# Tokens times the fused matrix: seven block products for each pair of token blocks in place of eight

## The chip, the cores and the metric

The kernel runs on one core of one Trainium2 chip. The metric is the device time of one execution in microseconds (us), the median of three runs. The core's engines are named as the profile names them: PE (TensorE, its matmuls) with PEld (its weight loads), DVE (VectorE), ACT (ScalarE), POOL (GpSimd) and SP (SyncE, which here issues nearly all DMAs).

## The reference, cut to what matters

Four residual layers follow one another on x, 32 sequences of 64 tokens of 1024 values. Every layer adds a linear map of the tokens, chosen or adapted by an index of the sequence:

```python
x = x + _L0_cond_ref(x, itok_B_0_15, L0_cond_weights)            # mixes the 64 tokens of a sequence, W = weights[index]
x = x + _L1_cond_ref(x, itok_B_0_15, L1_cond_W, lora_A, lora_B)  # x W1 + (x A[i]) B[i], rank 16
x = x + _L2_cond_ref(x, itok_B_0_2, L2_cond_W, lora_A, lora_B_w) # x W2' + (x A[j]) B' / 2, rank 32
x = x + _L3_cond_ref(x, itok_B_0_7, L3_cond_W, Wr, A, B)         # x W3' + gated low rank, top 2 of 8 experts
```

All layers but the gate are linear in x. The kernel uses this: it multiplies the weights together first and the tokens once by the result.

## The kernel before

**Number format.** Every fp32 operand of a matmul is kept as two fp32r tiles, `_hi` (ACT copies with rounding) and `_lo` (DVE subtracts `_hi` from the value). A product takes the three terms of `TERMS`: hi by hi, hi by lo, lo by hi.

**Front (to about 262 us).** From W2 and W3 (and A3, Wr beside it) the kernel makes the operand E, and from W1 and E the fused matrix M of 1024 x 1024 with the columns TB for the low-rank parts. This second product goes row block by row block (`rows`, ten of them: two of LoRA B, then eight of W1). One row block has three chunks of columns, 488, 448 and 384 wide, each into its own PSUM bank; ACT and DVE take each chunk out as hi and lo, directly into M and TB. The last row block's chunks end at about 252.6, 257.4 and 261.5 us.

**Token blocks (262 us to the end).** A block is 128 tokens, two sequences; there are 16. Two blocks (s = 0, 1) make one turn of the loop on every engine; the first two and the last two are written out. For each block PE runs:

- the wide product, 48 matmuls of 512 columns: two column halves, eight blocks of K, three terms, into banks 0 and 1 (`run`, L965);
- the narrow product for the next block, 24 matmuls of 232 columns, block by S, the columns of TB and of A1 chosen for the two sequences (`narrow`, L951). POOL's `select` chooses them by index;
- the mixing of tokens by BD (layer 0), of the narrow result (L977) and of the wide one (L1014), and small matmuls and transposes for the low-rank chain h1, h2, gates (L983 to L1002);
- sixteen matmuls of 512 columns that add it all up in banks 2 and 3 (L1009 to L1021).

ACT and DVE take results out of PSUM (`xm`, `xn`, `h1c`, `h2c`, gates), and copy the output to `ost`. SP, one queue in order, loads the tokens (`raw`), BD (`load_w0`), stores the output and loads `b1s`, the rows of LoRA B of the two sequences, from DRAM (`load_b1s`; the index is read into a register first). Each engine's order is the order of the code; semaphores alone tie them.

## Time and profile before

| | before |
|---|---|
| time, median of 3 runs | 560.11 us (560.01 to 560.23) |
| span of the profiled execution | 558.3 us |
| PE busy | 551.1 us, 99% of the span |
| DVE, ACT, POOL busy | 199.2, 133.7, 77.3 us |
| granted TensorE clock | full in all slices |

The profile times the span from the first to the last instruction of one execution; the timed runs are 1.8 us longer, which lies around the span. The profile gives each matmul of 512 columns some 0.40 us, but matmuls overlap: the distance from one start to the next says what one costs, and is read from the timeline.

### The profile page before, as it was taken

What the parts mean: (1) busy time and instruction counts of PE and PEld (TensorE: products, weight loads), DVE (VectorE), ACT (ScalarE), POOL (GpSimd) and SP (SyncE); (2) the same over time, 40 slices, a digit from 0 to 9 for tenths busy, and PEclk for the clock granted to TensorE, in tenths of its full rate; (3) what the DMA queues carried; (4) which work ended last, traced back from release to release, by engine and by line L of the source; (5) the groups of instructions that cost most, each with busy time, mean ns of one, the idle gap of its engine ahead of it and who ended that gap; (6) DMA issues with size and microseconds to landing.
All of it is one profiled execution on the core that took longest, in us unless ns stands there. A gap on an engine that the chain in (4) does not pass through costs nothing.

```text
span 558.3 us, 9078 instructions
## 1 busy us (share of the span) xinstructions
PE 551.1 (99%) x2898; PEld 491.9 (88%) x2898; DVE 199.2 (36%) x566; ACT 133.7 (24%) x274; POOL 77.3 (14%) x202
## 2 busy tenths in 40 slices
PE   7999999999999999999999999999999999999997
PEld 6999999999999999999888888888888888888885
DVE  4751312132322222213543344334444344435423
ACT  5541311121111111113222212221222122221211
POOL 2401000000000000004122122202220222022200
PEclk9999999999999999999999999999999999999999
DMA  8703020044131101001522132223312232223211
...
DMA packets 21834, 45.37 MB, mean 81 GB/s; under 512 B 8100, under 2 KB 12836, under 8 KB 21684
## 3 DMA queue, kind: packets, MB, share of 16 engines
...
q14 instruction: 10, 0.08, 0.1%
...
## 4 chain that ended last, share of the span: by engine, by line
PE 97%; DMA 1%; DVE 0%; SPq 0%; ACT 0%; issue 0%; POOL 0%
PE bank L965 32%; PE bank L931 26%; PE bank L889 19%; PE bank L951 8%; PE bank L1021 4%; PE bank L1014 4%; PE bank L1009 1%; PE bank L1010 1%; DMA w2raw<-in_w_dram 1%; PE bank L977 1%; PE bank L983 0%; PE bank L991 0%; PE bank L1002 0%; PE bank L987 0%; DVE w2s_lo L670 0%; ACT w2s_hi L542 0%
## 5 line engine op out<-in xcount | busy, mean ns | idle before, releaser
L965 PE MATMUL bank<-m_lo,xt_hi 128*128 128x512 f32 x256 | 103.0, 403 | 0.0
L965 PE MATMUL bank<-m_hi,xt_lo 128*128 128x512 f32 x256 | 101.3, 396 | 0.0
L965 PE MATMUL bank<-m_hi,xt_hi 128*128 128x512 f32 x256 | 100.2, 391 | 0.0
L931 PE MATMUL bank<-e_lo,w1t_hi 128*128 128x488 f32 (+2 forms) x240 | 86.9, 362 | 0.0
L931 PE MATMUL bank<-e_hi,w1t_hi 128*128 128x488 f32 (+2 forms) x240 | 86.8, 362 | 0.0
L931 PE MATMUL bank<-e_hi,w1t_lo 128*128 128x488 f32 (+2 forms) x240 | 86.7, 361 | 0.0
L889 PE MATMUL bank<-g_hi,w2s_hi 128*128 128x384 f32 (+1 forms) x192 | 64.7, 337 | 2.4 <-DVE w2s_lo L670 2.4
L889 PE MATMUL bank<-g_hi,w2s_lo 128*128 128x384 f32 (+1 forms) x192 | 64.5, 336 | 0.0
L889 PE MATMUL bank<-g_lo,w2s_hi 128*128 128x384 f32 (+1 forms) x192 | 64.5, 336 | 0.0
L965 PEld LDWEIGHTS bank<-m_lo,xt_hi 128*128 128x128 f32 x256 | 48.1, 188 | 10.7
L965 PEld LDWEIGHTS bank<-m_hi,xt_hi 128*128 128x128 f32 x256 | 48.3, 189 | 8.9
L965 PEld LDWEIGHTS bank<-m_hi,xt_lo 128*128 128x128 f32 x256 | 48.2, 188 | 8.6
L931 PEld LDWEIGHTS bank<-e_lo,w1t_hi 128*128 128x128 f32 x240 | 45.2, 188 | 3.9
L931 PEld LDWEIGHTS bank<-e_hi,w1t_hi 128*128 128x128 f32 x240 | 45.0, 188 | 4.0
L931 PEld LDWEIGHTS bank<-e_hi,w1t_lo 128*128 128x128 f32 x240 | 45.1, 188 | 3.9
L670 DVE TENSOR_TENSOR xm_lo<-bank,xm_hi 128x512 fp32r<-128x512 f32 x32 | 22.1, 692 | 72.2 <-ACT xm_hi L616 72.2
L670 DVE TENSOR_TENSOR m_lo<-bank,m_hi 128x384 f32 (+3 forms) x24 | 12.3, 513 | 83.8 <-ACT tb_hi L583 57.5
L889 PEld LDWEIGHTS bank<-g_hi,w2s_hi 128*128 128x128 f32 x192 | 36.0, 188 | 3.1 <-issue 3.1
L951 PE MATMUL bank<-s_hi,xt_hi 128*128 128x232 f32 x128 | 36.3, 283 | 0.0
L889 PEld LDWEIGHTS bank<-g_hi,w2s_lo 128*128 128x128 f32 x192 | 36.0, 188 | 0.0
L889 PEld LDWEIGHTS bank<-g_lo,w2s_hi 128*128 128x128 f32 x192 | 36.0, 188 | 0.0
L951 PE MATMUL bank<-s_lo,xt_hi 128*128 128x232 f32 x128 | 35.2, 275 | 0.0
...
## 6 DMA issues: line engine op xcount, KB each, us to landing
...
```

Source lines behind the costliest of these rows:

```text
L670: V.tensor_tensor(dst, src, f32(hi), ALU.subtract).then_inc(signal, 1)
L889: ins = nc.tensor.matmul(to[:, 0:w], lhs, G[c][z][:, k, 0:w], start=(k == 0 and n == 0), stop=(k == K - 1 and n == len(terms) - 1), skip_g ...
L931: ins = nc.tensor.matmul(stage_bank(u, j)[:, 0:WIDTH[c]], W1T[u][a][:, k, :], EX[c][z][:, k, :], start=(k == 0 and (a, z) == TERMS[0]), st ...
L951: ins = nc.tensor.matmul(bank[4][:, 0:SC], XT[s][a][:, k, :], S[z][:, k, :], start=(k == 0 and (a, z) == TERMS[0]), stop=(k == K - 1 and ( ...
L965: ins = nc.tensor.matmul(bank[c][:, :], XT[s][a][:, k, :], M[z][:, k, c * BANK:(c + 1) * BANK], start=(k == 0 and (a, z) == TERMS[0]), sto ...
L977: ins = nc.tensor.matmul(res[:, 0:SC], BD[s][a][:, :], XN[z][:, :], start=(a, z) == TERMS[0], stop=(a, z) == TERMS[-1], skip_group_check=True)
L1009: nc.tensor.matmul(bank[2 + c][:, :], h1T[:, :], b1s[s][:, halves[c]], start=True, stop=False, skip_group_check=True)
L1010: nc.tensor.matmul(bank[2 + c][:, :], h2T[:, :], b2s[:, halves[c]], start=False, stop=False, skip_group_check=True)
L1014: nc.tensor.matmul(bank[2 + c][:, :], BD[s][a][:, :], XM[z][:, halves[c]], start=False, stop=False, skip_group_check=True)
L1021: ins = nc.tensor.matmul(bank[2 + c][:, :], GHT[a][:, :], B3[z][:, halves[c]], start=False, stop=(a, z) == TERMS[-1], skip_group_check=True)
```

## The change

Token blocks are now taken in pairs b0, b1. Tokens (b0, b1) by the halves of K, and M by halves of K and of columns, are 2 x 2 blocks, and their product is made by Strassen's scheme in the form with fewer sums (Winograd's). Each of the seven products p1, p5, p6, p2, p7, p3, p4 is 12 matmuls (four blocks of K, three terms) of 512 columns.

- The right operands are b11, b21, b22 of M and four combinations t1 to t4. Row blocks of M leave PSUM unsplit (`rows_raw`), POOL forms the combinations from them in SBUF (`right_of`, `combine`), and ACT and DVE split the seven operands in pieces of up to 2048 columns after the last row's first chunk (`split_hi`, `split_lo`).
- The left operands are the two blocks and sums of their halves: POOL makes four sums of 512 columns for each pair in the tile `tmp` and in `raw[1]` (`first_sum`, `pair_sums`), ACT and DVE split each (`operand_hi`, `operand_lo`). The tiles are reused: CS is t1's and t3's left operand, then XM slot 0; XB's first half is also XM slot 1; `ost` 2 and 3 lie in XB.
- Three sums of products are made by DVE in PSUM between accumulations (`bank[BB]`, `bank[BD_]`, `bank[BC]`), with p1 and p5 copied to SBUF by ACT (`held_p1`, `held_p5`).
- The output is made tile by tile, four tiles of 128 x 512 for each pair, on two banks in turn; `b1s[0]` is needed by the tiles 0 and 1 of the last four steps of PE's pair. SP stores each tile, and loads b1s[0] of the next pair behind the store of tile 1, b1s[1] behind that of tile 3. A load of b1s is four DMAs, not eight, from a scratch copy with three parts.
- S keeps its layout, but the columns chosen by `select` come from unsplit TBA, so POOL splits them (two copies and two subtractions of 256 columns in place of four copies).

```diff
+            def pair_io(p, last):
...
+                    for s in range(2):
+                        sp.wait_ge(s_idx, 48)
+                        sp.wait_ge(s_bd, 2 * p + s + 1)
...
+                    for s in range(2):
+                        sp.dma_start(raw[s][:, :, :], x[bass.ds(2 * p + 2 + s, 1)].rearrange("a p k t -> p (a k) t")).then_inc(s_raw[s], 16)
+                for n, (s, c) in enumerate(TILES):
+                    sp.wait_ge(s_idx, 48)
+                    if n % 2 == 0:
+                        sp.wait_ge(s_ya, 2 * p + n // 2 + 1)
+                    else:
+                        sp.wait_ge(s_yd, 2 * p + n // 2 + 1)
+                    sp.dma_start(orows[bass.ds(2 * p + s, 1)].rearrange("a t d -> (a t) d")[:, c * BANK:(c + 1) * BANK], ost[n][:, :]
+                                 ).then_inc(s_st[n], 16)
+                    if n % 2 and not last:
+                        done = held(sp, 4 * p + n + 1)
+                        sp.wait_ge(s_idx, 48)
+                        sp.wait_ge(s_y, done)
+                        load_b1s(2 * p + 2 + s, s)
...
             pool.wait_ge(s_acc, ACC_A + ACC_B - 2)
+            pool.wait_ge(s_rd, 3 * LAST + 2)
+            pool.wait_ge(s_ra, 4 * LAST + 2)
             select(0)
-            diagonal(0, 0)
-            pool.wait_ge(s_acc, ACC_A + ACC_B - 1)
-            for s in range(2):
-                nc.gpsimd.memset(f32(b1s[s][:, D + C3:]), 0.0).then_inc(s_b1z, 1)
-            diagonal(0, 1)
-            pool.wait_ge(s_accl, ACC_A + OUT * (ROWS - 1) + OUT_AT[1])
...
+            row_there(LAST)
+            right_of(2, KH - 1)
+            pool.wait_ge(s_acc, ACC_A + ACC_B)
+            first_sum(0)
+            right_of(4, KH - 1)
+            nc.gpsimd.memset(f32(b1s[0][:, D + C3:]), 0.0).then_inc(s_b1z, 1)
+            pool.wait_ge(s_s0l, 1)
+            nc.gpsimd.memset(f32(b1s[1][:, D + C3:]), 0.0).then_inc(s_b1z, 1)
+            right_of(3, KH - 1)
+
+            def pair_sums(p, last):
+
+                r11, r12, r21 = raw[0][:, 0:KH, :], raw[0][:, KH:K, :], raw[1][:, 0:KH, :]
+                pool.wait_ge(s_raw[0], 16 * p + 16 * (ROWS // 2 + 1))
+                pool.wait_ge(s_opl, OPS * p + 2)
+                nc.gpsimd.tensor_tensor(tmp[:, :, :], tmp[:, :, :], r11, ALU.subtract).then_inc(s_sum, 1)
+                if isinstance(p, int) and p == 0:
+                    select(1)
+                pool.wait_ge(s_opl, OPS * p + 3)
+                nc.gpsimd.tensor_tensor(tmp[:, :, :], r12, tmp[:, :, :], ALU.subtract).then_inc(s_sum, 1)
+                pool.wait_ge(s_opl, OPS * p + 4)
+                nc.gpsimd.tensor_tensor(r21, r11, r21, ALU.subtract).then_inc(s_sum, 1)
+                if not last:
+                    select(2 * p + 2)
+                    first_sum(p + 1)
+                    select(2 * p + 3)
+                    diagonal(2 * p + 2, 0, 4 * p + 2)
+                    diagonal(2 * p + 3, 1, 4 * p + 4)
...
+                act.wait_ge(s_sum, 4 * p + 2)
+                if not first:
+                    act.wait_ge(s_st[0], 16 * p)
+                    act.wait_ge(s_st[1], 16 * p)
+                operand_hi(DS[0][:, :, :], tmp[:, :, :])
+                h1_t(b0, 0)
...
+                nc.scalar.activation(held_p1[:, :], bank[BA][:, :], ACT.Copy).then_inc(s_cp, 1)
+                act.wait_ge(s_raw[1], 16 * p + 16 * (ROWS // 2 + 1))
+                if first:
+                    act.wait_ge(s_tr, formed(3, KH - 1))
+                else:
+                    act.wait_ge(s_mix, 4 * p)
+                    act.wait_ge(s_st[2], 16 * p)
+                    act.wait_ge(s_st[3], 16 * p)
+                operand_hi(XB[0][:, :, :], raw[1][:, :, :])
+                if first:
...
+                act.wait_ge(s_wide, made + PRODUCT["p5"])
+                nc.scalar.activation(held_p5[:, :], bank[BC][:, :], ACT.Copy).then_inc(s_cp, 1)
+                act.wait_ge(s_sum, 4 * p + 4)
+                operand_hi(CS[0][:, :, :], raw[1][:, 0:KH, :])
+                if first:
+                    split_hi("b22", WHOLE)
+                exp_of(b0)
+                xn_hi(b1, YB)
+                act.wait_ge(s_sum, 4 * p + 3)
+                operand_hi(XB[0][:, 0:KH, :], tmp[:, :, :])
...
+            act.wait_ge(s_ra, 4 * KH)
+            act.wait_ge(s_rd, 3 * KH)
+            split_hi("b11", WHOLE)
+            act.wait_ge(s_tr, formed(1, KH - 1))
+            split_hi("t1", WHOLE)
+            act.wait_ge(s_rd, 3 * LAST + 1)
+            nc.scalar.activation(S[0][:, :, 0:C3], TBC[:, :, :], ACT.Copy).then_inc(s_s0h, 1)
+            rows_raw(ROWS - 1, 1, [1])
+            left_hi(0)
+            act.wait_ge(s_tr, formed(2, KH - 2))
+            split_hi("t2", FRONT)
+            act.wait_ge(s_ra, 4 * LAST)
+            act.wait_ge(s_rd, 3 * LAST)
+            split_hi("b21", FRONT)
+            split_hi("t3", FRONT)
+            rows_raw(ROWS - 1, 1, [2])
+            act.wait_ge(s_b2st, 16 * 3)
+            xn_hi(0, YB)
+            pair_hi(0, False)
+            with act.Fori(1, NP - 1) as p:
...
+
+                operand_lo(CS[1][:, :, :], tmp[:, :, :], CS[0][:, :, :], ops + 2)
+                if first:
+                    dve.wait_ge(s_tr, formed(4, KH - 1))
+                    split_lo("t2", BACK, SPLIT_HI["t2b"])
+                first_low_rank(b0, 0, steps)
+                operand_lo(DS[1][:, :, :], tmp[:, :, :], DS[0][:, :, :], ops + 3)
+                if first:
+                    split_lo("b21", BACK, SPLIT_HI["b21b"])
+                second_low_rank(b0, 0, steps)
+                operand_lo(XB[1][:, :, :], raw[1][:, :, :], XB[0][:, :, :], ops + 4)
+                if first:
+                    dve.wait_ge(s_tr, formed(3, KH - 1))
+                    split_lo("t3", FRONT, SPLIT_HI["t3a"])
+                route(b0, 0, steps)
+                operand_lo(CS[1][:, :, :], raw[1][:, 0:KH, :], CS[0][:, :, :], ops + 5)
+                dve.wait_ge(s_wide, made + PRODUCT["p6"])
+                dve.wait_ge(s_cp, 2 * p + 1)
+                V.tensor_tensor(bank[BB][:, :], bank[BB][:, :], held_p1[:, :], ALU.add).then_inc(s_add, 1)
+                if first:
+                    split_lo("t3", BACK, SPLIT_HI["t3b"])
+                dve.wait_ge(s_add, 3 * p + 1)
+                dve.wait_ge(s_cp, 2 * p + 2)
+                V.tensor_tensor(bank[BD_][:, :], bank[BB][:, :], held_p5[:, :], ALU.add).then_inc(s_add, 1)
+                gates(b0, 0, steps)
+                if first:
+                    split_lo("b22", WHOLE, SPLIT_HI["b22"])
+                xn_lo(b1, YB)
+                operand_lo(XB[1][:, 0:KH, :], tmp[:, :, :], XB[0][:, 0:KH, :], ops + 6)
+                first_low_rank(b1, 1, steps)
...
+            def tile(p, n, first, last):
+
+                s, c = TILES[n]
+                to, cols = bank[YB + n % 2], slice(c * BANK, (c + 1) * BANK)
+                above(pe, s_yd if n % 2 else s_ya, 2 * p + n // 2)
+                if n == 1 and not last:
+                    pe.wait_ge(s_xnl, 2 * p + 3)
+                pe.wait_ge(s_xml, 4 * p + n + 1)
+                for a, z in TERMS:
+                    ins = nc.tensor.matmul(to[:, :], BD[s][a][:, :], XM[n % 2][z], start=(a, z) == TERMS[0], stop=False, skip_group_check=True)
+                ins.then_inc(s_mix, 1)
+                nc.tensor.matmul(to[:, :], h1T[s][:, :], b1s[s][:, cols], start=False, stop=False, skip_group_check=True)
+                nc.tensor.matmul(to[:, :], h2T[s][:, :], b2s[:, cols], start=False, stop=False, skip_group_check=True)
+                pe.wait_ge(s_ghl, 2 * p + s + 1)
+                if first and n == 0:
+                    pe.wait_ge(s_b3l, 1)
...
+                there("b11")
+                part("p1", 0, 5)
+                mixed(b0, 0)
+                part("p1", 5, 11)
+                h1_across(b0, 0)
+                part("p1", 11, 12)
+                pe.wait_ge(s_opl, OPS * p + 2)
+                there("t1b")
+                part("p5", 0, 3)
+                h1_into(b0, 0, p)
+                part("p5", 3, 11)
+                h2_across(b0, 0)
+                part("p5", 11, 12)
+                pe.wait_ge(s_opl, OPS * p + 3)
+                there("t2b")
+                part("p6", 0, 4)
                 if first:
...
+                h2_into(b0, 0)
+                part("p6", 4, 12)
+                pe.wait_ge(s_opl, OPS * p + 4)
+                narrow(b1, XB, YB)
+                pe.wait_ge(s_cp, 2 * p + 1)
+                there("b21b")
+                part("p2", 0, 6)
+                mixed(b1, 1)
+                part("p2", 6, 12)
+                gated_across(b0, 0)
+                pe.wait_ge(s_add, 3 * p + 2)
+                pe.wait_ge(s_opl, OPS * p + 5)
+                there("t3b")
+                part("p7", 0, 1)
+                h1_across(b1, 1)
+                part("p7", 1, 6)
+                h1_into(b1, 1, p)
+                part("p7", 6, 12)
+                pe.wait_ge(s_opl, OPS * p + 6)
+                there("b22")
+                part("p3", 0, 2)
+                h2_across(b1, 1)
+                part("p3", 2, 8)
+                h2_into(b1, 1)
+                part("p3", 8, 12)
+                pe.wait_ge(s_add, 3 * p + 3)
+                there("t4")
+                part("p4", 0, 12)
...
+            pe.wait_ge(s_rd, 3 * LAST + 3)
+            pe.wait_ge(s_ra, 4 * LAST + 2)
+            pe.wait_ge(s_ml, SPLIT_LO["b11"])
+            pe.wait_ge(s_s0l, 1)
+            pe.wait_ge(s_opl, 1)
+            nc.tensor.matmul(bank[BD_][:, :], XA[0][:, 0, :], MO["b11"][0][:, 0, :], start=True, stop=True, skip_group_check=True)
+            narrow(0, XA, YB)
```

Where POOL's program passes from the front to the token blocks, it had this order before (behind two reads of `idx_a` S is filled for block 0, then BD, then the spare columns of b1s are cleared):

```order
L475 ISA [waits s_id]
L475 COPY s_hi<-a1raw 128x8x16
L475 ISA
L475 COPY s_hi<-a1raw 128x8x16
L485 TENSOR_TENSOR s_lo<-a1raw,s_hi 128x8x16 [waits s_a1c,s_id]
L485 TENSOR_TENSOR s_lo<-a1raw,s_hi 128x8x16
L456 TENSOR_TENSOR bdraw_100<-bdraw_100,ident 128x128 [waits s_w00]
L461 CAST bd_hi<-bdraw_100 128x128 [waits s_bdc,s_id]
L463 TENSOR_TENSOR bd_lo<-bdraw_100,bd_hi 128x128 [waits s_bdc]
L496 MEMSET b1s_132 96x64 [waits s_acc]
```

and has this now, behind four reads of `idx_a` and `idx_l` and two copies from `tba` (`tba` holds the unsplit columns, `mr_left`, `mr_right` and `tr` the parts of M and t1 to t4, `tmp` the tokens' sum):

```order
L527 COPY s_hi<-a1raw 128x8x16
L527 ISA
L527 COPY s_hi<-a1raw 128x8x16
L531 TENSOR_TENSOR s_lo<-tba,s_hi 128x8x32 [waits s_a1c,s_id]
L531 TENSOR_TENSOR s_lo<-tba,s_hi 128x8x32
L531 TENSOR_TENSOR s_lo<-a1raw,s_hi 128x8x16 x2
L534 TENSOR_TENSOR tr_54<-mr_right,tr_53 128x512 [waits s_tr,s_rd,s_ra]
L556 TENSOR_TENSOR tmp<-raw_115 128x512 [waits s_raw1,s_acc]
L534 TENSOR_TENSOR tr_56<-mr_left,tr_54 128x512 [waits s_tr]
L580 MEMSET b1s_161 96x64
```

Two index reads became four, the first `select` fills and splits all columns of S, and b1s is cleared only behind three operations of 512 columns.

SP's order at the end of a block before (one store, then b1s for the block after the next one, which is used a whole block later):

```order
L400 DMA out_dram<-ost_96 128x1024 [waits s_yfree1,s_yfree0]
L349 TENSOR_LOAD idx_a
L349 ISA x2
L349 TENSOR_LOAD idx_l
L349 ISA x2
L366 ISA
L366 DMA b1s_132<-b1scr 32x1160
L366 ISA
L366 DMA b1s_132<-b1scr 32x32
L366 DMA b1s_132<-b1scr 16x1160
L366 DMA b1s_132<-b1scr 16x32
```

and now at the end of a pair behind the store of tile 1 and two index reads (`ost_172` and `ost_173` are the tiles 2 and 3; b1s 161 is that of the next pair's first block):

```order
L416 DMA b1s_161<-b1scr 48x32
L400 TENSOR_LOAD idx_a
L400 ISA x2
L400 TENSOR_LOAD idx_l
L400 ISA x2
L416 ISA
L416 DMA b1s_161<-b1scr 48x1160
L416 ISA
L416 DMA b1s_161<-b1scr 48x32
L452 DMA out_dram<-ost_172 128x512 [waits s_ya,s_idx]
L452 DMA out_dram<-ost_173 128x512 [waits s_yd,s_idx]
```

Between the stores of tile 1 and tile 2 there is now a whole load of b1s with its index reads, and the block that needs it follows at once.

DVE in the middle of a pair in the loop now (`held_p` are the copies of p1 and p5; `den` and `gw` begin the gates; before, no instruction of DVE wrote to a `bank`):

```order
L841 TENSOR_TENSOR cs_lo<-raw_115,cs_hi 128x512 [waits s_oph]
L1053 ISA
L1055 TENSOR_TENSOR bank<-bank,held_p_174 128x512 [waits s_cp,s_wide]
L1058 ISA
L1059 REGISTER_ALU [waits s_add]
L1060 TENSOR_TENSOR bank<-bank,held_p_175 128x512 [waits s_cp]
L1018 TENSOR_SCALAR den<-ex 128x1 [waits s_ex]
L972 REGISTER_ALU
L1020 RECIPROCAL gw<-den 128x1 [waits s_dc]
```

The two sums stand between the split of the next left operand and the gates; the low half of `xn`, which PE waits for, comes behind the gates.

## Rows read from the trace of the kernel before

**Rows 1.** The page: busy time of each engine, and granted clock by slices.
```profile
PE 551.1 (99%) x2898; PEld 491.9 (88%) x2898; DVE 199.2 (36%) x566; ACT 133.7 (24%) x274; POOL 77.3 (14%) x202
...
PEclk9999999999999999999999999999999999999999
```

**Rows 2.** The page: chain that ended last, by engine.
```profile
PE 97%; DMA 1%; DVE 0%; SPq 0%; ACT 0%; issue 0%; POOL 0%
```

**Rows 3.** Windows view, one pair in the loop: length, then each engine's busy time.
```profile
374.24:410.90 36.66, 36.66 (x194) 30.91 (x193) 15.14 (x52) 8.47 (x19) 7.92 (x22) 1.00 0.26 84
```

**Rows 4.** Groups by line and form: one of three wide groups of 256.
```profile
L965 PE MATMUL bank<-m_lo,xt_hi 128*128 128x512 f32 x256 | 103.0, 403 | 0.0
```

**Rows 5.** Timeline, PE: start, length, line, operation; wide product, then narrow one.
```profile
382.42 0.39 PE L965 MATMUL bank<-m_hi,xt_lo 128*128 128x512 f32 x1
...
386.05 0.27 PE L951 MATMUL bank<-s_hi,xt_hi 128*128 128x232 f32 x1
...
388.83 0.40 PE L1009 MATMUL bank<-b1s,h1T 96*128 96x512 f32 x1
```

**Rows 6.** Timeline, PE: a transpose put between wide matmuls.
```profile
395.21 0.27 PE L983 MATMUL bank<-ident,h1c 128*96 128x128 f32 x1
...
395.55 0.39 PE L965 MATMUL bank<-m_hi,xt_lo 128*128 128x512 f32 x1
```

**Rows 7.** Timeline, SP's DMA issues: store, then eight b1s loads.
```profile
393.77 0.39 SPq L400 DMA_DIRECT2D out_dram<-ost  x1
396.16 5.07 SPq L366 DMA_DIRECT2D b1s<-b1scr  x8
```

**Rows 8.** Timeline, SP: first issue of the second half of these.
```profile
399.40 0.90 SPq L366 DMA_DIRECT2D b1s<-b1scr  x2
```

**Rows 9.** Line L349, SP's reads of an index: ns min/median/max.
```profile
L349 SPq TENSOR_LOAD <-idx_l x32: 262/270/867, 259.4 to 527.7; - x32
```

**Rows 10.** DMA view: issues, KB each, median us to landing.
```profile
out_dram<-ost SPq DMA_DIRECT2D x4, 256.0 KB, 2.1
...
b1s<-b1scr SPq DMA_DIRECT2D x32, 2.0 KB, 1.9
```

**Rows 11.** Groups by form, DVE and ACT: count, busy us, mean ns.
```profile
L670 DVE TENSOR_TENSOR xm_lo<-bank,xm_hi 128x512 fp32r<-128x512 f32 x32 | 22.1, 692 | 72.2 <-ACT xm_hi L616 72.2
...
L670 DVE TENSOR_TENSOR xt_lo<-raw,xt_hi 128x1024 fp32r<-128x1024 f32 x16 | 20.0, 1251 | 0.7 <-ACT xt_hi L604 0.2
L616 ACT ACTIVATE xm_hi<-bank 128x512 fp32r<-128x512 f32 x32 | 19.1, 597 | 59.5 <-PE bank L965 59.5
L604 ACT ACTIVATE xt_hi<-raw 128x1024 fp32r<-128x1024 f32 x16 | 16.8, 1051 | 0.0
```

**Rows 12.** Timeline, DVE: first and last step of a block's gates.
```profile
382.77 0.15 DVE L826 TENSOR_SCALAR den<-ex 128x1 f32<-128x1 f32 x1
...
384.07 0.29 DVE L837 TENSOR_TENSOR gh<-bank,gate 128x128 f32<-128x128 f32 x1
```

**Rows 13.** Timeline, POOL: end of one `diagonal`, then a `select`.
```profile
283.31 0.46 POOL L463 TENSOR_TENSOR bd_lo<-bdraw,bd_hi 128x128 fp32r<-128x128 f32 x1
286.26 0.53 POOL L475 CAST s_hi<-a1raw 128x128 fp32r x2 [2.49 <-issue]
...
288.13 0.88 POOL L485 TENSOR_TENSOR s_lo<-a1raw,s_hi 128x128 fp32r<-128x128 f32 x2
```

**Rows 14.** Timeline, POOL, 254.7 to 256.2 us.
```profile
254.53 1.29 POOL L475 CAST s_hi<-a1raw 128x128 fp32r x1
```

**Rows 15.** Timeline, DVE, in the same stretch.
```profile
254.36 1.30 DVE L670 TENSOR_TENSOR xt_lo<-raw,xt_hi 128x1024 fp32r<-128x1024 f32 x1 [0.21 <-ACT xt_hi L604]
```

**Rows 16.** Timeline, ACT: the last row's first two chunks leave PSUM.
```profile
252.75 0.38 ACT L583 ACTIVATE m_hi<-bank 128x256 fp32r<-128x256 f32 x1 [4.85 <-PE bank L931]
...
257.62 0.49 ACT L583 ACTIVATE m_hi<-bank 128x384 fp32r<-128x384 f32 x1 [2.28 <-PE bank L931]
```

**Rows 17.** Timeline, PE: the first narrow product begins.
```profile
261.54 0.27 PE L951 MATMUL bank<-s_hi,xt_hi 128*128 128x232 f32 x1
```

734 lines of the change are left out of this document (406 added, 328 removed).

## Prediction

> **What bounds the kernel now.** I read the page first. PE is busy for 99% of the span at the full granted clock in every slice, and no other engine passes 36% [rows 1]; the chain that ended last lies on PE for 97% [rows 2]. So time goes where PE's matmuls go, and the question is what one costs. The groups give 403 ns for a wide matmul, and there are three such groups of 256, 768 in all [rows 4]. That is not its price: in the timeline 16 wide matmuls start between 382.42 and 386.05, one each 0.227 us [rows 5]. The narrow product behind them, 24 matmuls and one transpose, takes 2.78 us, 0.111 each [rows 5]. A transpose put between wide matmuls makes two starts 0.34 apart where one matmul is 0.227, so it costs 0.11 [rows 6]. One turn of the loop, two blocks, is 36.66 us, in which PE is never free while DVE is busy for 15.1, ACT for 8.5, POOL for 7.9 [rows 3]. The reader is to see two things: every matmul less is worth its 0.227 us, and a wait of PE that is absent today costs its full length.
>
> **The change part by part.** I count in us and sum against the span of 558.3; the median of the timed runs, 560.1, lies 1.8 above it, which I keep.
>
> *Removed: 96 wide matmuls.* 12 of 96 in each of eight pairs, 96 x 0.227 = 21.8 less. Nothing else on PE changes in number: narrow, mixing, small products and the four tiles of eight matmuls are as many as before; one matmul is added ahead of the first narrow product (0.2). Without waits a pair would take 36.66 - 2.73 = 33.9.
>
> *Unseen prices.* DVE's sums into PSUM: nearest rows are the subtraction from PSUM, 0.69, and ACT's copy, 0.60 [rows 11]; I take 0.70 each, bounds 0.6 and 1.25 (the row of 1024 columns). POOL's two-input operation of 512 columns: the row has 0.44 each at 128 columns (two in 0.88) [rows 13]; were all of it fixed cost, 0.44, were none, 1.76; a part of an operation this short is fixed, as on DVE (0.69 for 512 columns, 1.25 for 1024), so I take 1.3, with 0.16 fixed, and 0.72 at 256 columns. Splits of 512 columns: 0.6 on ACT and 0.65 on DVE, half and a little of the rows of 1024, 1.05 and 1.25; 2048 columns: 2.0 and 2.4 [rows 11]. DVE's load stays under PE's: 15.1 + 3 x 0.7 + 4 x 0.65 = 19.8 in 34.
>
> The Trainium skill's GPSIMD Engine Reference, section 3.1, gives 4497 ns for a two-input add of 2048 columns; a quarter would be an estimate of 1.1, and with it the waits below would be 0.2 shorter for each such operation in their chain. No row here has that size.
>
> *POOL and DVE block each other.* A POOL copy that takes 0.29 otherwise began at 254.53 and took 1.29; DVE had begun a subtraction with both inputs in SBUF at 254.36, which ran to 255.66 [rows 14, 15]. So such an operation of DVE holds POOL up to its end. The Trainium skill's SBUF — State Buffer, section Who interferes with whom, states this as a lock held for a whole instruction; by that rule, the trace agrees. The change puts many more such operations on both.
>
> *A steady pair, seven of them: first wait.* Let a pair begin at 0. PE reaches `h1_into(b0)` after p1 (12 matmuls), 3 narrow ones, a transpose and 3 matmuls of p5: 15 x 0.227 + 0.33 + 0.11 = 3.85. It needs b1s[0]. The old tile is read by the previous pair's tile 1, which ends 3.65 before 0 (two tiles of eight at 0.23); DVE's copy of it ends at -2.7. SP then stores it (0.2), the first b1s issue comes 2.4 after the store's [rows 7], the second 0.6 later; the second half began 3.24 after the first issue behind four issues [rows 7, 8], with two fewer 2.4; its last issue is 0.6 on and lands 1.9 later [rows 10]: -2.7 + 0.2 + 2.4 + 2.4 + 0.6 + 1.9 = 4.8. Wait 1.0. Before, the same load had a whole block of 18 us. Bounds 0 and 2.
>
> *Second wait.* Behind that load, in SP's queue, tiles 2 and 3 are stored, the latter at 3.9, landing at 6.0 [rows 10]. XB lies in their place, so ACT's split waits: 6.0 + 1.05 (ACT) + 1.25 (DVE) + 1.3 (POOL, r11 - r21) + 0.6 + 0.65 (CS) + 1.4 (two sums) + 1.6 (gates, 382.77 to 384.36 [rows 12]) + 0.4 (xn) + 0.4 for handing on = 14.65. PE wants xn for `mixed(b1)` after p1, p5 and p6 with their small matmuls (36 x 0.227 + 0.8 = 9.0), the narrow product (2.7) and six matmuls of p2 (1.35), at 13.0, and now 14.0 by the first wait. Wait 0.65, bounds 0 and 1.5. In all 1.65 x 7 = 11.5 (bounds 0 and 21 with the dearest prices). Queued behind PE's wait is everything, since nothing else can be begun.
>
> *Front to first pair.* Count from 252.75, where the last row's first chunk is taken [rows 16]. The second is out of PE at 4.9; the first narrow product began at 8.8 [rows 16, 17]. Now ACT splits b11, t1 (2.0 each) and S (1.1) first and takes the second chunk by 5.7. Only then does POOL read four indices, 2.5 (the issue time ahead of a `select` [rows 13]), and fill S. A `select` took 2.75 (286.26 to 289.01 [rows 13]); two copies of 256 turn into subtractions: 3.5. That is 11.7 with POOL alone; with the two DVE splits of 1536 columns (1.8) that fall in between, 15. Then t2's part, `first_sum` and t4's part (3.9), a split of DVE between (0.65): 19.5. Then b1s is cleared and SP needs 6.3 to load it (as above, without the store: 1.5 of index reads, 2.4 + 0.6 + 1.9): 25.8. PE would want it at 8.8 + 2.7 + 3.85 = 15.4. Lost 10.4; without the blocking 7.3; with all of it 11.6.
>
> *First pair, behind that.* From `h1_into(b0)` PE wants xn of b1 9.15 later. POOL has `select(1)` and two sums left, DVE XB and t3 to split, each blocking the other: r11 - r21 is done at 6.7 (5.2 without blocking, 8.1 with all). Then CS 1.25, two sums 1.4, t3's rest 0.65, gates 1.6, b22's low half 2.4, xn 0.4, handing on 0.3: 14.7. Lost 5.6 (4.2 to 8.4). Together 16.0, bounds 11.5 and 20.
>
> *The rest:* the last pair has no narrow product ahead of its tiles, so PE meets DVE's gates: 0.3; 0.2 for the added matmul. The row stage is left at nothing: the two chunks left at 252.75 are done when the narrow product begins at 261.54, 8.8 [rows 16, 17], a whole row about 14, and POOL's three operations (3.9) lie in it; if that cover went, they would be 4 per row.
>
> *Sum.* -21.8 + 11.5 + 16.0 + 0.5 = +6.2: span 564.5, time 566.3.
>
> **The rivals.**
>
> *Faster: the waits stay small.* If b1s lands before PE asks, the steady pair loses 0.3 at most (2 in all), and the start loses only 11.5: -21.8 + 2 + 11.5 + 0.5 = -7.8, time 552.3. For it: both steady waits are differences of about 1 us between sums of ten terms; SP's reads of `idx_l` take 0.27 as a rule and 0.87 at most [rows 9], and a read of the longer kind would explain why 2.4 passed ahead of the first issue; 0.6 less removes half of the first wait. Against it: SP's order can't be got round, and the first narrow product depends on POOL behind ACT. It decides once all waits together stay under 21.
>
> *Much slower: PE's clock falls.* PE would stand idle for 6 us ahead of its first narrow product. Every stretch here has the full 2.4 GHz [rows 1], as PE was never idle so long, so no row prices a fall. If the stretch up to the second wait of the first pair (13 us of work) ran at 1.2 GHz, half of it lies in the first wait anyway; 5 more: 571. The Trainium skill's TensorE: Matmul & The Clock Gate, section What's actually happening, says that an idle array falls back to half clock; by that rule this would happen here, and no run shows it yet.
>
> *No change from it:* the sevenfold scheme might gain nothing if PE were held by loading weights, or DVE became the bound. PEld was busy for 30.9 of 36.66 [rows 3], but with the same ratio of loads to matmuls now, and DVE has 14 us to spare. Nearly excluded; 560.
>
> **How the numbers follow.** The measurement tells 0.2% (1.1 us) from no change. Chances: forecast 0.50, its own range 560 to 573, of which 0.05 falls within 0.2%; faster rival 0.36, 0.02 of it within; clock 0.10; no change 0.04, of which 0.01 within. Hence faster 0.35, same 0.08, slower 0.57. The bounds of the unknown prices give -21.8 + 11.5 + 0.5 = -9.8 (550) and -21.8 + 21 + 20 + 0.5 = +19.7 (580), both with everything at one end; for eight in ten I cut to 551 and 576. The predicted time is that of the likeliest case, 566.3.
>
> **What would show it.** In the profile after: 672 matmuls of the seven products at the same distance of 0.227; PE waiting for POOL's S or index reads ahead of the first narrow product; PE waiting for the b1s DMA at each b0, 1 us, and for xn_lo at each b1; a loop turn of 35.6. It would be wrong if a turn were near 33.9 with PE never idle (then 552 or less), if POOL's 512 columns took nearer 0.9, or if a slice with a lower granted clock appeared.

## The result: 572.0 us, 2.1% slower, twice the loss forecast

The changed kernel takes 572.0 us (571.4 to 573.7), the kernel before 560.1 in the same session: a ratio of 1.0212, 95% interval 1.0195 to 1.0228. Forecast were 566.3, so the direction was right, and +12.0 stands where +6.2 was said. The profiled execution has a span of 570.3 against 558.3.

The page of the changed kernel, its busy time and granted clock by slices (beside [rows 1]), and its chain (beside [rows 2]):

```profile
PE 540.0 (95%) x2803; PEld 478.6 (84%) x2803; DVE 252.1 (44%) x611; ACT 165.0 (29%) x318; POOL 162.7 (29%) x254
...
PEclk8999999999999999998889999999999999999999
...
PE 73%; issue 10%; POOL 6%; DVE 5%; ACT 1%; POOLq 1%; DMA 1%; SPq 1%; DVEq 0%; ACTq 0%
```

PE has less to do, 540 us, but now it waits: 30 us of the span are not PE's, where 7 were. POOL and DVE have entered the chain, and three slices, 257 to 299 us, show a granted clock of 8 where there was no fall before (the first slice of the span shows 8 too; nothing below rests on it). PE's waits, summed by line and releaser (total, times, longest):

```profile
PE bank L1216 <- DVE xn_lo L841: 10.2, 7, 6.5
PE bank L1228 <- DMA b1s<-b1scr: 5.9, 8, 0.9
PE bank L1192 <- POOL s_lo L531: 5.8, 1, 5.8
```

These are the three waits that the prediction named: `mixed(b1)` for xn_lo, `h1_into(b0)` for b1s, the first narrow product for S. PE's timeline at the turn to the pairs, in the first pair, and in one turn of the loop (start, length, line, idle time ahead):

```profile
262.24 0.40 PE L1331 MATMUL bank<-b_hi,w1t_hi 128*128 128x512 f32 x1
268.41 0.56 PE L1192 MATMUL bank<-s_hi,w1t_hi 128*128 128x232 f32 x1 [5.78 <-POOL s_lo L531]
268.77 0.41 PE L1192 MATMUL bank<-s_lo,w1t_hi 128*128 128x232 f32 x1
268.98 0.41 PE L1192 MATMUL bank<-s_hi,w1t_lo 128*128 128x232 f32 x1
...
279.18 0.33 PE L1228 MATMUL bank<-b1s,h1T 96*128 96x200 f32 x1 [0.86 <-DMA b1s<-b1scr]
...
296.14 0.53 PE L1216 MATMUL bank<-xn_hi,bd_hi 128*128 128x232 f32 x1 [6.45 <-DVE xn_lo L841]
...
297.78 0.63 PE L1206 MATMUL bank<-b_hi,w1t_lo 128*128 128x512 f32 x1
298.20 0.63 PE L1206 MATMUL bank<-b_hi,w1t_hi 128*128 128x512 f32 x1
...
431.30 0.36 PE L1228 MATMUL bank<-b1s,h1T 96*128 96x200 f32 x1 [0.64 <-DMA b1s<-b1scr]
441.43 0.35 PE L1216 MATMUL bank<-xn_hi,bd_hi 128*128 128x232 f32 x1 [0.62 <-DVE xn_lo L841]
```

The reader is to look at the starts, not at the lengths. Behind the wait of 5.78 the narrow matmuls start 0.21 apart, where [rows 5] has 0.11; behind the wait of 6.45 the wide ones start 0.42 apart, where it has 0.227. That is half speed: 1.2 GHz instead of 2.4. Between the two, from 274 to about 290, the clock is full. Windows of the changed kernel (length, busy time of PE, PEld, DVE, ACT and POOL, the mean granted clock, then the DMA share and GB/s):

```profile
252.00:262.00 10.00, 10.00 (x54) 9.44 (x53) 7.39 (x8) 8.41 (x8) 2.98 (x7) 1.00 0.00 1
262.00:274.00 12.00, 6.22 (x29) 5.84 (x28) 5.09 (x4) 2.45 (x5) 11.71 (x14) 0.72 0.00 0
274.00:290.00 16.00, 13.88 (x73) 10.59 (x72) 11.85 (x23) 7.67 (x13) 12.49 (x14) 1.00 0.33 95
290.00:303.00 13.00, 6.86 (x23) 5.49 (x24) 9.87 (x20) 4.38 (x8) 4.26 (x7) 0.74 0.21 81
303.00:340.00 37.00, 35.47 (x187) 29.34 (x185) 22.20 (x64) 11.72 (x25) 14.59 (x26) 1.00 0.26 85
```

The chain behind the second wait of a loop turn begins where the prediction put it, at the landing of tile 3's store; ACT's row, 6.0 behind the first product of its pair:

```profile
432.62 1.06 ACT L706 ACTIVATE xb_hi<-raw 128x1024 fp32r<-128x1024 f32 x1 [1.72 <-DMA out_dram<-ost]
```

**Where the 12 us are.** I cut both traces at the last row's first chunk on ACT, at the first product of the second pair, and at the end. Before: 252.75 [rows 16], 300.97, 558.3. After: 253.38, 319.39, 570.3. So 0.6 is there at the first cut; the turn and the first pair take 66.0 instead of 48.2 (+17.8); the other seven pairs take 250.9 instead of 257.3 (-6.4). Sum +12.0. Forecast for the three parts: 0, +13.5 (16.0 + 0.2 - 2.7) and -7.2. The term that was mis-sized is the first pair, by 4.3; then come 0.8 in the other pairs and 0.6 in the row stage. The last is no effect of the change that I can show: in the profiles of the twelve experiments the row stage ends between 260.9 and 263.8, with the same code on PE.

### The profile page after: what moved, and what is told of

The parts are those of the page before. It is cut to its first block, busy times and chain, and to the rows that moved or that the text cites. A ratio compares the mean times of both kernels' runs of the same rounds, so it can differ in the third digit from the quotient of the medians.

```text
span 570.3 us, 9106 instructions
## 1 busy us (share of the span) xinstructions
PE 540.0 (95%) x2803; PEld 478.6 (84%) x2803; DVE 252.1 (44%) x611; ACT 165.0 (29%) x318; POOL 162.7 (29%) x254
## 4 chain that ended last, share of the span: by engine, by line
PE 73%; issue 10%; POOL 6%; DVE 5%; ACT 1%; POOLq 1%; DMA 1%; SPq 1%; DVEq 0%; ACTq 0%
PE bank L1174 25%; PE bank L1128 19%; PE bank L1206 15%; PE bank L1192 5%; PE bank L1254 4%; PE bank L1262 3%; POOL tmp L594 2%; POOL raw L596 2%; POOL tmp L590 1%; PE bank L1257 1%; PE bank L1256 1%; ACT cs_hi L706 1%; PE bank L1216 1%; DVE bank L1055 1%; POOL s_lo L531 1%
## 5 line engine op out<-in xcount | busy, mean ns | idle before, releaser
L841 DVE TENSOR_TENSOR w1t_lo<-raw,w1t_hi 128x1024 fp32r<-128x1024 f32 x18 | 23.2, 1288 | 60.0 <-ACT w1t_hi L631 60.0
L841 DVE TENSOR_TENSOR e_lo<-bank,e_hi 128x384 fp32r<-128x384 f32 (+1 forms) x24 | 13.3, 561 | 61.8 <-ACT e_hi L666 61.8
L527 POOL CAST s_hi<-tba 128x256 fp32r x32 | 16.1, 531 | 83.9 <-PE bank L1192 76.5
L1128 PEld LDWEIGHTS bank<-g_lo,w2s_hi 128*128 128x128 f32 x192 | 36.5, 190 | 0.0
L687 ACT ACTIVATE mr_left<-bank 128x384 f32 (+3 forms) x16 | 6.2, 385 | 86.2 <-PE bank L1174 86.2
L666 ACT ACTIVATE e_hi<-bank 128x384 fp32r<-128x384 f32 (+1 forms) x24 | 11.9, 495 | 65.4 <-PE bank L1128 65.2
L534 POOL TENSOR_TENSOR tr<-mr_right,mr_left 128x512 f32<-128x512 f32 x4 | 5.2, 1295 | 81.2 <-DMA b1scr<-b1stage_hi 45.6
L494 POOL DMA_DIRECT2D b2scr<-b2stage x3 | 1.8, 597 | 92.5 <-DVE b2stage L841 92.5
L531 POOL TENSOR_TENSOR s_lo<-tba,s_hi 128x256 fp32r<-128x256 f32 x32 | 26.6, 854 | 2.4 <-POOL s_hi L527 1.4
L1206 PE MATMUL bank<-t_hi,cs_hi 128*128 128x512 f32 x64 | 26.5, 413 | 0.0
L1206 PE MATMUL bank<-b_hi,w1t_lo 128*128 128x512 f32 x64 | 26.4, 413 | 0.0
```

The lines of the kernel that those rows point to most:

```text
L527: nc.gpsimd.tensor_copy(S[0][:, :, at_:at_ + n], src).then_inc(s_a1c, 1)
L531: nc.gpsimd.tensor_tensor(S[1][:, :, at_:at_ + n], src, f32(S[0][:, :, at_:at_ + n]), ALU.subtract).then_inc(s_sel, 1)
L666: nc.scalar.activation(EX[c][0][:, ob, 0:w], bank[n % 6][:, 0:w], ACT.Copy).then_inc(s_acch, 1)
L841: V.tensor_tensor(dst, src, f32(hi), ALU.subtract).then_inc(signal, 1)
L1128: ins = nc.tensor.matmul(to[:, 0:w], lhs, G[c][z][:, k, 0:w], start=(k == 0 and n == 0), stop=(k == K - 1 and n == len(terms) - 1), skip_g ...
L1206: ins = nc.tensor.matmul(to[:, :], left[a][:, k0 + k, :], right[z][:, k, :], start=(name in OPENS and n == 0), stop=(n == 3 * KH - 1), ski ...
```

## The experiments

All of them keep the seven products. For each, PE's timeline gives two lengths: A, from the end of the row stage to `mixed(b0)` of the second pair (the turn and the first pair), and the usual turn of the loop. The row stage's own scatter is in neither. Ratios are to the kernel before, run on the same chip; where the chips differ they say more than the times. All in us. The steps of PE named below: `mixed` needs xn_lo, `h1_across`, `h2_across` and `gated_across` transpose h1c, h2c and gh, the result of the gates, and `h1_into` is the product with b1s.

```
kernel                       A     turn   time    ratio  (95% interval)
before                      40.6   36.6   560.1
after                       58.3   35.7   572.0   1.0212 (1.0195 1.0228)
e1  xn_lo before the gates  56.2   36.5   576.5   1.0267 (1.0234 1.0300)
e2  SP's entries read early 58.3   35.15  568.9   1.0126 (1.0083 1.0169)
e3  PE busy, 26 + 28        57.8   35.8   572.9   1.0204 (1.0171 1.0237)
e3b PE busy, 26 + 9         54.1   35.8   567.6   1.0145 (1.0125 1.0166)
e4  DVE's splits wait       56.7   35.8   571.0   1.0173 (1.0137 1.0208)
e5  POOL's entries early    56.4   35.7   570.9   1.0204 (1.0183 1.0225)
e6  mixed(b1) later         56.9   35.2   567.1   1.0132 (1.0103 1.0162)
e7  POOL's selection later  56.9   35.6   571.6   1.0202 (1.0182 1.0222)
e8  seven edits together    53.5   34.3   558.3   0.9969 (0.9956 0.9982)
e9  and the first pair      52.7   34.3   557.2   0.9937 (0.9920 0.9955)
e10 and PE busy again       53.5   34.3   557.8   0.9952 (0.9932 0.9973)
e11 e9 without e7's edit    52.6   34.3   557.2   0.9946 (0.9929 0.9962)
```

A comes from one execution each, and about 1 us of it is chance in the clock. In the changed kernel, e1, e2 and e6 all 24 narrow products behind the wait for S start 0.21 apart, 5.0 from first to last. In e7 nothing that runs up to there was changed, and the wait is the same, 5.77; yet the last nine start 0.11 apart:

```profile
267.68 0.56 PE L1193 MATMUL bank<-s_hi,w1t_hi 128*128 128x232 f32 x1 [5.77 <-POOL s_lo L531]
...
270.60 0.41 PE L1193 MATMUL bank<-s_lo,w1t_hi 128*128 128x232 f32 x1
270.82 0.36 PE L1193 MATMUL bank<-s_hi,w1t_lo 128*128 128x232 f32 x1
271.01 0.27 PE L1193 MATMUL bank<-s_hi,w1t_hi 128*128 128x232 f32 x1
271.12 0.27 PE L1193 MATMUL bank<-s_lo,w1t_hi 128*128 128x232 f32 x1
```

`mixed(b0)` stands 5.5 behind the first of them, 6.6 in the changed kernel. The clock came back as early in e5 and e8 (4.1 and 4.2 from first to last).

**PE kept busy in its two long waits (e3, e3b).** My theory is that the forecast's rival "PE's clock falls" took part, in addition to the waits; the rival theory is that the waits alone cost. The added products write a bank that nobody reads at that time.

```diff
+            for _ in range(27):      # was once
             nc.tensor.matmul(bank[BD_][:, :], XA[0][:, 0, :], MO["b11"][0][:, 0, :], start=True, stop=True, ...)
             narrow(0, XA, YB)
...
                 part("p2", 0, 6)
+                if first:
+                    pe.wait_ge(s_cp, 2)
+                    for _ in range(28):      # e3b: 9
+                        nc.tensor.matmul(bank[BC][:, :], DS[0][:, 0, :], MO["b21"][0][:, 0, :], start=True, stop=True, ...)
                 mixed(b1, 1)
```

> Edit: TensorE gets added 128x512 products whose results are not used, in the two long waits of the first pair: 26 before the first narrow product (into the bank that is only opened there) and 28 before the second block's mixed product. They take the waits' time and no more. Theory (part of the loss is TensorE's granted clock, which falls in these two waits): the 23 to 30 products after each wait run at 0.23 and 0.11 us again instead of 0.44 and 0.22. Behind the second wait that gives 2.7 us; behind the first the 2.6 us go into the wait for b1s at h1_into. Sum 572.0 - 2.7 = 569.3. Rival (the waits alone cost, the slow products stood beside other waits anyway): 572.0 within 0.5. Rival (clock worth both stretches): 566.7.

Measured 572.9, and this looked like the rival. But in its trace xn_lo was ready at 293.3 and the 28 added products ran to 297.6. So the second wait had shrunk and I had filled it past its end. Hence the second run:

> Edit: as the run with 26 and 28 unused products, but 9 instead of 28 in the second wait. There xn_lo(b1) was done at 293.3 and TensorE's unused products ran until 297.6, so 4.2 us of the first pair was my filler, not the kernel's. Theory (the fall of the granted clock costs time, through the 24 narrow products behind the first wait as well): mixed(b1) starts at 293.4 instead of 296.1 and what follows runs at full clock: 572.9 - 4.1 = 568.8. Rival (the clock costs nothing, another wait takes its place): 571 to 573.

Measured 567.6 (the intervals of the two ratios, 1.0125 to 1.0166 and 1.0195 to 1.0228, don't meet); A is 54.1, which is 4.2 less than in the changed kernel. Its windows over the turn, the stretch between, and the second wait:

```profile
261.00:273.00 12.00, 12.00 (x66) 9.75 (x64) 7.00 (x7) 4.05 (x8) 11.85 (x14) 1.00 0.01 1
273.00:289.00 16.00, 12.36 (x61) 10.15 (x61) 11.83 (x29) 7.51 (x13) 10.92 (x16) 0.89 0.44 128
289.00:302.00 13.00, 11.56 (x53) 8.64 (x52) 11.52 (x23) 5.47 (x9) 6.07 (x6) 1.00 0.10 40
```

PE's timeline in e3b, with the nine added products in one row and the product behind them, then the next wait:

```profile
288.88 2.26 PE L1301 MATMUL bank<-b_hi,ds_hi 128*128 128x512 f32 x9
291.85 0.35 PE L1216 MATMUL bank<-xn_hi,bd_hi 128*128 128x232 f32 x1 [0.71 <-DVE xn_lo L841]
...
298.33 0.33 PE L1233 MATMUL bank<-ident,h2c 128*128 128x128 f32 x1 [0.73 <-DVE h2c L996]
```

The clock is full in the two stretches that had 0.72 and 0.74; it dips to 0.89 between them, where the wait for b1s still is. Of the 4.2, the stretch from `mixed(b1)` to the next pair gives 1.2 (23.2 instead of 24.4; some more went into a new wait for h2c, 0.73), and 3.0 come before it: that was not expected. I had written the first fall off, since the wait for b1s lies behind it. It does reappear there (2.35 in place of 0.86). But the 24 slow narrow products also delayed xn_lo(0) (`mixed(b0)` stands 10.2 behind the row stage in e3b, 12.8 in the changed kernel), and DVE works in order: behind xn_lo(0) stand CS's split, on which POOL's next sum waits, and so on to the gates. A at 54.1 is +13.5 over before, the sum that the forecast had without a fall of the clock; given the scatter of about 1 us, that it agrees to the tenth is luck. The two fillings were not run one by one: the 3.0 and the 1.2 are read from the timeline.

**VectorE's splits wait for S (e4).**

```diff
             dve.wait_ge(s_tr, formed(4, KH - 2))
+            dve.wait_ge(s_sel, 4)
             split_lo("t2", FRONT, SPLIT_HI["t2a"])
```

> Edit: at the turn from the front to the pairs VectorE's splits of t2 and b21 (front parts, 1.75 and 1.95 us) wait until GpSimd has finished the selection of S for block 0. Theory (GpSimd's two casts of S took 3.46 us instead of 1.23 because VectorE's subtractions ran beside them): the casts take 1.2 us, S is there 2.2 us sooner, PE's first narrow product starts at 266.2 instead of 268.4, b1s and everything behind move with it if the splits of VectorE do not become late: 572.0 - 2.2 = 569.8. Rival (no contention, the casts wait for something else): casts stay at 3.4 us, time 572 or more, up to 575 because the splits are late.

A fell by 1.6, the time by 1.0, by the ratios 2.2 (the intervals overlap). The start of the first narrow product comes 3.45 behind the row stage instead of 6.17, 2.7 sooner. POOL's timeline in the changed kernel:

```profile
262.04 3.46 POOL L527 CAST s_hi<-tba 128x256 fp32r x2 [6.63 <-issue]
265.45 0.53 POOL L527 CAST s_hi<-a1raw 128x128 fp32r x2
```

POOL's in e4:

```profile
261.35 0.74 POOL L527 CAST s_hi<-tba 128x256 fp32r x2 [6.64 <-issue]
...
264.90 1.28 POOL L534 TENSOR_TENSOR tr<-mr_right,tr 128x512 f32<-128x512 f32 x1
266.14 2.80 POOL L556 TENSOR_TENSOR tmp<-raw 128x512 f32<-128x512 f32 x1
268.90 2.78 POOL L534 TENSOR_TENSOR tr<-mr_left,tr 128x512 f32<-128x512 f32 x1
```

DVE's in e4:

```profile
265.04 2.76 DVE L841 TENSOR_TENSOR t_lo<-tr,t_hi 128x1536 fp32r<-128x1536 f32 x1 [4.03 <-POOL s_lo L531]
267.72 2.83 DVE L841 TENSOR_TENSOR b_lo<-mr_left,b_hi 128x1536 fp32r<-128x1536 f32 x1
```

The same two casts take 0.74 with DVE silent and 3.46 beside its subtractions. The postponed work then met POOL's sums: the sum of 512 columns, 1.29 alone, takes 2.80, and DVE's 1536 columns take 2.8 instead of 1.75. The ends of the five rows alternate: POOL 266.18, DVE 267.80, POOL 268.94, DVE 270.55, POOL 271.68. Each instruction is done only 1.1 to 1.6 behind the end of the other engine's, so the two take turns, and each lasts about as long as both alone (1.28 + 1.75 = 3.0). So the 2.7 won at S shrank to 1.6 at the pair's end. The clock fell here too (the narrow products start 0.11 apart behind a wait of 3.06, from the fourteenth on 0.21); whether that has a part in the loss isn't shown.

**POOL's table entries and b1s's clearing early (e5).**

```diff
+            select(0, sources_there)      # reads its four entries, then waits for the columns
+            pool.wait_ge(s_acc, ACC_A + ACC_B)
+            nc.gpsimd.memset(f32(b1s[0][:, D + C3:]), 0.0).then_inc(s_b1z, 1)
             row_there(LAST)
             right_of(2, KH - 1)
-            pool.wait_ge(s_acc, ACC_A + ACC_B)
             first_sum(0)
             right_of(4, KH - 1)
-            nc.gpsimd.memset(f32(b1s[0][:, D + C3:]), 0.0).then_inc(s_b1z, 1)
...
```

> Edit: GpSimd reads the four table entries of block 0 ahead of its waits for the last row's columns, and clears b1s right behind the selection instead of behind three sums. Theory (S of block 0 and b1s are late because of GpSimd's order): the first cast starts at 259.0 instead of 262.0, S is there about 3 us sooner, the b1s load starts 6 us sooner and h1_into(b0) no longer waits: it comes at about 276 instead of 279.2, and the rest of the first pair with it. 572.0 - 3 = 569.0. Rival (VectorE's three subtractions at 259 to 263 hold GpSimd's casts whenever they start, S comes at 267 or later): 571 to 572.

A fell by 1.9, not 3; the time by 1.1, by the ratios 0.5, within the intervals. About 1 of the 1.9 is the clock that came back sooner, which this edit can't be credited with. The wait for b1s in the first pair is gone, but S came only 0.65 sooner (a gap of 5.52 ahead of the first narrow product where there were 6.17): the casts started sooner and stood beside DVE's subtractions longer. The rival was right about S.

**xn_lo ahead of the gates (e1).**

```diff
+                xn_lo(b1, YB)
                 gates(b0, 0, steps)
                 if first:
                     split_lo("b22", WHOLE, SPLIT_HI["b22"])
-                xn_lo(b1, YB)
```

> Edit: on VectorE, in every pair, the split of the second block's narrow product (xn_lo) goes ahead of the first block's gates instead of behind them. Theory (waits in VectorE's order): in the loop of the changed kernel mixed(b1) waits for xn_lo, about 0.8 us of lost start per pair; the split could start when its high part is there, 0.8 us sooner, so 7 pairs give 5.5 us. In the first pair the low half of b22 (2.28 us) still stands ahead of the first low-rank step of block 1, so of its 6.8 us only about 2.4 come back, and the wait moves to the transpose h1_across. Sum 572.0 - 7.9 = 564, turn 34.9 us. Rival (VectorE is too full in that stretch, the later gates make gated_across wait): turn stays 35.6, time 570 or more.

This fell: 576.5, the turn 36.5 instead of 34.9. The first pair did as said (A 2.1 less). DVE in one turn of e1:

```profile
441.83 0.40 DVE L841 TENSOR_TENSOR xn_lo<-bank,xn_hi 128x232 fp32r<-128x232 f32 x1 [0.83 <-ACT xn_hi L718]
...
442.82 0.92 DVE L1025 TENSOR_SCALAR gm<-iota,topf,gw 128x8 f32<-128x8 f32 x2
443.78 0.66 DVE L1027 TENSOR_TENSOR gate<-gm 128x8 f32<-128x8 f32 x1
```

DVE had nothing to do for 0.83 ahead of xn_lo, where it used to do half of the gates. The wait for xn_lo goes, and two others come in every turn, PE idle for 0.39 ahead of gated_across and for 0.66 ahead of h1_across: starts 0.78 and 1.16 apart instead of 0.23, so 1.5 lost in place of 0.8. The split was not late because it stood behind the gates; the gates filled a gap.

**mixed(b1) six products later (e6).**

```diff
-                part("p2", 0, 6)
-                mixed(b1, 1)
-                part("p2", 6, 12)
+                part("p2", 0, 12)
                 gated_across(b0, 0)
+                mixed(b1, 1)
...
-                part("p7", 0, 1)
+                part("p7", 0, 4)
                 h1_across(b1, 1)
-                part("p7", 1, 6)
+                part("p7", 4, 9)
                 h1_into(b1, 1, p)
...
```

> Edit: on TensorE mixed(b1) comes behind all 12 products of p2 instead of behind 6, and the steps on it in p7 and p3 three products later. Theory (xn_lo is late for where mixed(b1) stands, and there is slack behind it): the wait of 0.8 us per pair in the loop goes, 7 x 0.8 = 5.5 us, and 1.4 us in the first pair: 572.0 - 6.9 = 565.1, turn 34.9 us. Rival (as with the split ahead of the gates, the wait comes back at h1_across or h2_into or at the gates of block 1): turn 35.4 or more, 570 or more.

Measured 567.1; A 1.4 less as said, the turn 35.2. The wait for xn_lo is gone from the loop. Of its 0.8 per turn 0.5 are gained; h1_across waits about 0.15 (starts 0.38 apart), and b1s 0.15 more (0.79 idle in the turn at 428 against 0.64).

**SP's entries read early (e2).**

```diff
                     if n % 2 == 0:
+                        chosen = None if last else b1s_rows(2 * p + 2 + s)
                         sp.wait_ge(s_ya, 2 * p + n // 2 + 1)
...
-                        load_b1s(2 * p + 2 + s, s)
+                        load_b1s(2 * p + 2 + s, s, chosen)
```

> Edit: SyncE reads the table entries for the next b1s load ahead of its wait for the first of the two output stores, instead of between the store of tile 1 and the load. Theory (the b1s load starts late because of what SyncE does between the two stores and the load): issue moves about 2 us earlier, h1_into(b0) no longer waits; 0.8 us of lost start in each of 7 pairs, so 572.0 - 5.6 = 566.5, turn 34.9. Rival (the load is held by the tiles' last reads of the old b1s, not by SyncE's own work): issue moves under 0.5 us, time 571 to 572.

Measured 568.9, turn 35.15. SP's issues in one turn of the changed kernel:

```profile
422.01 2.43 SPq L452 DMA_DIRECT2D out_dram<-ost  x2
426.19 3.26 SPq L416 DMA_DIRECT2D b1s<-b1scr  x4
```

And in one turn of e2:

```profile
420.82 2.47 SPq L456 DMA_DIRECT2D out_dram<-ost  x2
423.69 2.04 SPq L419 DMA_DIRECT2D b1s<-b1scr  x4
```

Counted from the first store the four loads begin 1.3 sooner and end 2.5 sooner. The wait for b1s is gone from the loop, as the theory had it; but of its 0.8 only 0.5 is gained, since the next wait in the pair, for xn_lo, grew from 0.62 to 0.86. The trace shows why, in SP's queue: the entries of the second load are now read ahead of the stores of tiles 2 and 3, which therefore start only 0.2 sooner in the turn (1.74 behind `mixed(b0)` instead of 1.97), and XB's split, with which the chain to xn_lo begins, 0.3 sooner.

**POOL's selection later (e7).**

```diff
                 if not last:
+                    pool.wait_ge(s_h1c, 4 * p + 4)
                     select(2 * p + 2)
```

> Edit: alone, on the changed kernel: GpSimd's selection for the next pair waits until VectorE has formed block 1's first low-rank step; today it starts when narrow(b1) is done and runs beside block 0's gates. Theory (the gates, and with them xn_lo, are slowed by GpSimd's work beside them: the pair of gate steps takes 0.81 us there and 0.48 us without): xn_lo comes 0.35 us sooner in each pair and about 0.9 us sooner in the first: 572.0 - 3.3 = 568.7, turn 35.3. Rival (the two engines do not disturb each other in such small steps, the length is VectorE's own): 571 to 572, turn 35.6, the step stays at 0.8.

The mechanism is right and the gain is not there: 571.6, turn 35.6. (A is 1.4 less, but 1.0 of it is there before the edit acts, by the clock.) DVE in one turn of e7:

```profile
437.51 0.48 DVE L1026 TENSOR_SCALAR gm<-iota,topf,gw 128x8 f32<-128x8 f32 x2
...
447.03 1.30 DVE L1013 CAST topf<-topi 128x2 f32<-128x2 uint32 x1
```

The gate step takes 0.48 beside a silent POOL, against 0.81 in the changed kernel. The wait for xn_lo shrinks by about 0.5. But POOL's selection and sum now fall later, a two-column cast of DVE beside them takes 1.30 (0.17 in the changed kernel's turn), the next pair's left operand is split later, and the narrow product (0.2) and b1s (0.2) wait for what was won.

**Together (e8), and more of the first pair (e9, e10, e11).** e8 has the edits of e2, e4, e5, e6 and e7; two more on DVE in the first pair: t3's split waits for `select(1)`, b22's goes behind block 1's first low-rank step.

> Edit: seven together: SyncE's table entries read ahead of its waits; GpSimd's entries of block 0 read ahead and b1s cleared early; mixed(b1) behind all of p2; GpSimd's selection for the next pair waits for block 1's first low-rank step; in the first pair VectorE's splits of t2 and b21 wait for S of block 0, that of t3 for S of block 1, and that of b22 goes behind block 1's first low-rank step. Theory (all that the change lost are waits from order): turn 34.0 us, so 7 x 1.6 = 11.2 us; first pair 3 + 2.3 + 3 us shorter: 572.0 - 19.5 = 552.5. Rival (as these waits go, others come: VectorE or GpSimd holds the turn near 35): 560 or more.

Measured 558.3, ratio 0.9969: faster than the kernel before by 0.3%, but 5.8 short of the sum. The turn is 34.3, and a usual turn has no start later than 0.16 beyond the ordinary. Two waits of 0.8 gave 0.5 each alone and 1.35 together (e11 shows that e7's edit has no part in it): each had hidden part of the other. Most of the missing part is the first pair: 4.8 instead of 8.3 off A; the rest is the turn, 34.3 instead of 34.0. PE's waits in e8:

```profile
PE bank L1255 <- DVE gh L1039: 3.1, 2, 3.0
...
PE bank L1204 <- POOL s_lo L537: 2.2, 1, 2.2
PE bank L1228 <- DVE xn_lo L851: 2.2, 1, 2.2
PE bank L1245 <- DVE h2c L1006: 1.7, 2, 1.5
```

e9 adds 11 unused products in the wait for S, puts DVE's split of b21's front part behind block 0's low-rank steps and XB's split, and POOL's b22 - b12 behind its second sum; e10 adds 8 unused products in the wait for gh; e11 is e9 without e7's edit.

> Edit: on the seven together: 11 unused products while TensorE waits for S of block 0; VectorE's split of b21 (front part, 2.82 us where it stands now) goes behind the sums of the first steps of block 0; GpSimd's b22 - b12 goes behind the second of its token sums. Theory (the first pair has a chain of its own: S, xn_lo(0), the sums, the gates, each late because something not yet needed stands ahead): the 24 narrow products end 2.5 us sooner, xn_lo(0) no longer waits behind two splits, and the pair ends about 3 us sooner: 558.3 - 3 = 555.3. Rival (VectorE and GpSimd are full together in that stretch, moving work only moves the wait to the gates): 558.

> Edit: as the run before it, and 8 unused products while TensorE waits for block 0's gates in the first pair (3.4 us there in the seven together, products behind it at up to 0.45 us). Theory (clock): another 1 us, 554.3. Rival (a wait of 3 us is too short to lower the clock, or the products behind it stand beside other waits): as the run before it, within 0.5.

> Edit: the run with the first pair's order changed (557.2), but GpSimd's selection for the next pair starts again when narrow(b1) is done. Alone that hold moved nothing (turn 35.6 with it and without). Theory (waits in one queue hide each other: with the b1s wait and the xn_lo wait gone, VectorE's slowed gates do count): turn 34.7 instead of 34.3, 557.2 + 3 = 560. Rival (the hold is worth nothing; the turn of 34.3 comes from SyncE's early reads and the later mixed product alone, whose 0.5 and 0.5 us are larger together): turn 34.3, 557.

e9: 557.2, A only 0.8 less. The narrow products do end sooner, but the pair now waits longer where DVE and POOL are both full; its wait for gh is 3.0 as before. The rival was nearer. e10: nothing (557.8, intervals overlap). In e9 the products behind the wait of 3.0 start 0.43 apart; in e10 they start 0.23 apart, but the next wait, for h2c, is 2.5 instead of 1.5, and behind it the starts are 0.43 apart. e11: 557.2, turn 34.3, so the rival is right and e7's edit is worth nothing alone or with the others. e9 and e11 can't be told apart; the simpler e11 is what I would keep, 0.5% (0.4 to 0.7) faster than the kernel before.

## Why the prediction was right in sign and off in size

- *Removed work:* right. 672 wide matmuls start 0.23 apart, and with the loop's waits gone the turn is 34.3 (e8), near the 33.9 of the forecast.
- *A steady pair:* right in places and prices. The turn was forecast at 35.6 and is 35.6 to 35.8, 36.0 in the second pair. The lost starts are 0.8 and 0.8 (a gap of 1.05 and 1.01 less the usual 0.23) where 1.0 and 0.65 were said. e2 and e6 confirm both causes. What the sum did not say is that the gains of removing them don't add up.
- *Unseen prices:* POOL's 512 columns were put at 1.3 and take 1.28 to 1.29 undisturbed, DVE's sums into PSUM at 0.70 and take 0.69. The Trainium skill's GPSIMD Engine Reference, section 3.1, has 4497 ns for 2048 columns; a quarter of that, an estimate of 1.1, is lower than the trace.
- *Front to h1_into(b0):* forecast 25.8 us behind the last row's first chunk; measured 253.38 to 279.18, 25.8. Here one error was covered: the narrow products ran at half speed (5.3 instead of 2.7), and the wait for b1s took it up.
- *First pair, behind that:* the mis-sized term, "Lost 5.6 (4.2 to 8.4)". From h1_into(b0) to the end of xn_lo(b1) 14.7 were forecast and 16.8 passed; from there to the next pair the products ran at half speed until about 301 and took 2.4 more than in the loop (24.4 against 22.0), for which the forecast had nothing. That is 4.5 more, 10.1 in all, beyond the upper bound. e3b shows that 4.2 of the turn and first pair hang on the granted clock: 3.0 up to `mixed(b1)`, by the delay of DVE's queue, and 1.2 behind it.
- *The rivals:* "PE's clock falls" had the cause right and came near in size (5, measured 4.2) and in its sum, 571, with a chance of 0.10. The place is right only in part, so the nearness is partly luck: it put the whole stretch from the first wait to the second, 13 us of work, at 1.2 GHz, while the trace has the clock full again at 274, 5.3 us behind the end of the first wait, and a second fall behind the second wait. The chance was mis-sized: a wait of 6 us was in the forecast itself, and the fall was treated as an alternative to it and not as what follows from it. The Trainium skill's TensorE: Matmul & The Clock Gate, section What's actually happening, has an idle array fall back to half clock; the trace agrees (0.72 and 0.74 in the windows of the two waits). "Faster" was wrong as a forecast of this kernel, yet its condition, all waits under 21 us, is the way that e8 to e11 go.
- *What stays open:* of the 0.8 that the other seven pairs lost beyond the forecast 0.4 is the second pair's turn, the rest is spread over some 0.1 per turn; neither was traced further. Nor were e8's gains in the first pair taken apart edit by edit, and when the clock comes back behind the same wait differs from run to run without a cause that the traces show.
